# Loading the first fifteen pieces of two edge tables at stated counts of landed scatter groups

## The chip, the cores and the metric

The kernel runs on one core of a Trainium2 chip. The metric is the device time of one execution, in microseconds (us). The kernel before takes 2910.95 us, the median of 3 runs (2910.61 to 2911.79).

## The reference

Four stages stand one behind the other, each with a residual and a layer norm ahead of it: a graph network of three layers (SAGE with batch norm), an attention over learned slices, a hypergraph convolution, and a mixture of eight experts. The graph has 3125 nodes of 256 features and 53125 directed edges, sorted by target node. The change lies in the first graph layer, layer 0:

```python
for Wl, bl, Wr, g, b in params:
    agg = segment_sum(h[src], dst, N)
    deg = segment_sum(ones, dst, N)
    out = (agg / max(deg, 1)) @ Wl + bl + h @ Wr
    h = relu(batch_norm(out, g, b))
```

## The kernel before, in words

**Sums as products.** A neighbour sum h[src] by dst is a product of the features with a table of edge counts: 3200 x 3200 entries in fp16, source nodes by target nodes. The targets are split into five blocks of 640 (`NB` = 5, `BC` = 640), and a block of the table into five pieces (q = 0 to 4), each with the counts of 640 sources, 800 KB. The index n = 5b + q numbers the pieces through the blocks.

**Making the table.** There are two tables in DRAM, `at_counts` (even) and `odd_counts` (odd), so that two groups of scatters can be under way. VectorE works out, for groups of 512 edges, an address and a count for each (line 1147), and POOL writes them with DMAs that add one count per partition: four scatters of 128 make a group (`add_group`, line 602), even groups go to the even table, odd ones to the odd. There are 104 groups, 52 for each table. Ahead of a group of a table POOL waits until the table's previous group has landed (`pool.wait_ge(added, g // 2 * GROUP)`; `GROUP` = 64 is what one landed group adds to the semaphore `even_added` or `odd_added`). Since the edges are sorted by target, a block of the table is complete once a certain number of groups has landed.

**Using it.** SP's queue loads the pieces. `released(k, b)` reads the number of groups that block b needs, worked out from the edges by the kernel, and waits for it, once per table and block. Then for each piece `load_even(n)` fetches the even table's into `ring` (one of five slots; `chunk_used[q]` says that the slot is free, `sum_out` that what stood there was stored), and `load_odd(n)` the odd table's into one of two slots in `xrows` (`tables_summed` says that the slot is free). VectorE adds the two (`sum_tables`, line 1254), ACT's queue stores the sum back to the even table for the later layers (line 786), and TensorE multiplies (`aggregate`: degrees at line 1951, features at 1959). After a block's five pieces VectorE divides by the degrees (`aggregated`, lines 1213 to 1229), TensorE applies the weights (`mean_products`, line 1977) and VectorE adds and collects statistics (lines 1236, 1203).

**Order.** SP's queue loads nothing before all 104 groups have been worked out (`sp.wait_ge(idx_ready, NG)`), since `ring` holds the keys until then. All queues run in written order. VectorE's is: the five sums of block 0; then, for each block b, the sums n = 5(b+1) and 5(b+1)+1 of the next block, the division for block b, the sum of q = 2, the first of four additions, the sum of q = 3, the other three additions and the statistics, the sum of q = 4. TensorE enters block b+1 when the four additions of block b are done. The last block is loaded and used in three parts, each with its own release (targets 2560 to 2879, 2880 to 2996, and the rest; lines 1261 to 1301 on VectorE, 2013 to 2041 on TensorE). Layer 1 begins when the last part has gone through the batch norm.

Of the kernel before, what the change touches and what calls it, by code (L numbers as in the profile page):

```python
# [12 lines left out]
NB = T // BT  # L13
# [21 lines left out]
CHECKS = 3  # L35
EARLY = 4
GROUP = GQ * 16
AROW = T * BC
SPREAD = 64
ZW = 2000  # L40
AHEAD = BT + 3
ASIZE = NB * P * AROW
EPS = 1e-5
# [61 lines left out]
def build(nc, x, src, dst, w, out):  # L105
    ctx = ExitStack()
    with ctx:
# [65 lines left out]
        tfeat = tarena[:, 0:4 * T * P].rearrange("p (f n) -> p f n", f=4)  # L173
        zeros16 = tarena[:, :].bitcast(fp16)[:, 0:AROW]
        deginv = late[:, :]
# [142 lines left out]
        compared, idx_ready, even_added, odd_added, tables_summed = map(sem, ("compared", "idx_ready", "even_groups_added", "odd_groups_added", "tables_summed"))  # L318
# [117 lines left out]
        def _(sp):  # L436
# [22 lines left out]
            def released(k, b):  # L459
                landed = sp.value_load(release[:, k, b:b + 1], min_val=GROUP, max_val=NG * GROUP)  # L460
                sp.nop(nofuse=True)
                sp.wait_ge((even_added, odd_added)[k], landed)
                sp.nop(nofuse=True)

            def load_even(n):
                b, q = n // NB, n % NB
                sp.wait_ge(chunk_used[q], b + 1)
                if n >= NB:
                    sp.wait_ge(sum_out[(n - NB) % 2], 16 * ((n - NB) // 2 + 1))
                sp.dma_start(chunk_flat[q], at[:, b, q * BT * BC:(q + 1) * BT * BC]).then_inc(chunk_in[q], 16)  # L470

            def load_odd(n):
                b, q = n // NB, n % NB
                if n >= 2:
                    sp.wait_ge(tables_summed, n - 1)
                sp.dma_start(odd_chunk[n % 2], odd[:, b, q * BT * BC:(q + 1) * BT * BC]).then_inc(odd_in[n % 2], 16)

            for b in range(NB - 1):
                released(0, b)
                released(1, b)  # L480
                for q in range(NB):
                    load_even(b * NB + q)
                    load_odd(b * NB + q)
# [80 lines left out]
        def _(pool):  # L564
# [31 lines left out]
            def add_group(g, table, added):  # L596

                pool.wait_ge(idx_ready, g + 1)
                if g >= 2:
                    pool.wait_ge(added, g // 2 * GROUP)  # L600
                for c in range(g * GQ, (g + 1) * GQ):
# [92 lines left out]
        def _(act):  # L694
# [11 lines left out]
            def clear(table, zeroed, b):  # L706
                act.dma_start(table[:, b, :].rearrange("p (k c) -> p k c", c=ZW), zeros16[:, 0:ZW].unsqueeze(1).to_broadcast([P, AROW // ZW, ZW])).then_inc(zeroed, 16)

# [196 lines left out]
            def block_sqrt(b):  # L905
                wait(ln_var, 5 + NB + b)
                tiles = slice(b * BT, b * BT + BT)
                nc.scalar.activation(ln_s[:, tiles], ln_r[:, tiles], ACT.Sqrt).then_inc(ln_std, 1)

            _, c_tps, c_tcp, c_xps, c_high, _ = conv  # L910

            def conv_copy(t, i, k):
# [84 lines left out]
        def _(dve):  # L997
# [9 lines left out]
            def step(ins):  # L1007

                o.mark(ins)
                o.settle()  # L1010
# [9 lines left out]
            o.mark(V.tensor_reduce(row_block, eflt[:, 3, :], AX.X, ALU.max))  # L1020
            step(V.tensor_scalar(ekeyT, eflt[:, 0, :], float(AROW), None, ALU.mult))
            step(V.scalar_tensor_tensor(out=ekeyT, in0=eflt[:, 2, :], scalar=float(BC - P * AROW), in1=ekeyT, op0=ALU.mult, op1=ALU.add))
            step(V.scalar_tensor_tensor(out=ekeyT, in0=eflt[:, 3, :], scalar=float(P * AROW - BC), in1=ekeyT, op0=ALU.mult, op1=ALU.add))
            V.tensor_tensor(ekeyT, ekeyT, eflt[:, 1, :], ALU.add).then_inc(keys_dve, 1)
# [92 lines left out]
            def block_releases():  # L1117
# [19 lines left out]
                step(V.tensor_tensor(release[:, 0, :], groups, odd_groups, ALU.subtract))  # L1137
                V.tensor_scalar(release[:, 0:2, :], release[:, 0:2, :], GROUP, None, ALU.mult).then_inc(keys_dve, 1)
                dve.wait_ge(keys_dve, 5)
# [686 lines left out]
        def _(pe):  # L1826
# [62 lines left out]
            def enter_block(l, b, tile_rows, weights, last=HB):  # L1889

                rows, _, lo = ent[l][0:3]
                for h, tiles in ((0, (0, 1)), (1, (2, 3, 4))):
                    for i in tiles:
                        pe.wait_ge(lo, b * BT + (2 if i == 4 else 1))
                        for f in range(4):
                            if i == tiles[0]:
                                pe.wait_ge(rows, b * 8 + (4 * h + f + 1))
                            ins = tile_rows(i, f)
                        ins.then_inc(ent[l][3], 1)
                    half_products(l, b, h, weights, HB if h == 0 else last)  # L1900
# [305 lines left out]
            def turned(b, i, rows, tps, tcp, base=0):  # L2206
# [5 lines left out]
                ins.then_inc(tps, 1)  # L2212

            c_rows, c_tps, c_tcp, c_xps, _, c_low = conv

            def conv_turn(t, i, k):
# [192 lines left out]
```

## Time and profile before

| | us |
|---|---|
| median of 3 timed runs | 2910.95 |
| lowest, highest | 2910.61, 2911.79 |
| profiled execution, span from first to last instruction | 2916.6 |
| TensorE (PE) busy | 2404.2 |
| VectorE (DVE) busy | 1066.9 |
| POOL busy | 874.0 |
| ACT busy | 450.7 |

The profile is of one further execution, and nothing of it but its span is given as a time; it isn't one of the three that were timed. A busy time is the sum over an engine's instructions; waiting, and the issuing of DMAs by SP and ACT, aren't in it. POOL's scatters are counted as busy while POOL issues them; how long the data take to land is seen only by what waits for them. "Granted clock" is TensorE's clock as a share of 2.4 GHz. In a timeline, "idle before" in brackets is the time that the engine stood still ahead of an instruction, with what ended it; "issue" means that nothing the profile shows was waited for.

### The profile page before, as it was taken

The page shows a single profiled execution, that of the slowest core. Times are in us where ns is not written, and L with a number is a line of the kernel's source. Part 1 is how long each engine was busy: PE and PEld are TensorE (multiplying, and loading weights), DVE is VectorE, ACT ScalarE, POOL GpSimd, SP SyncE. Part 2 cuts the span into 40 slices and gives each one's busy share as a digit, 9 for nine tenths or more (in the row PEclk, how much of TensorE's full clock was granted, in tenths as well). Part 3 has the DMA queues.
Part 4 walks back from the last instruction along what each step waited for, and adds up shares of the span by engine and source line. Part 5 has one row for each costly group of instructions (what it writes and reads, how often), then busy time and mean ns, then how long its engine had stood idle before and what let it go on. Part 6 is the DMA issues. An engine that isn't in the chain of part 4 may idle for free.

```text
span 2916.6 us, 40191 instructions
## 1 busy us (share of the span) xinstructions
PE 2404.2 (82%) x14486; PEld 1802.4 (62%) x14486; DVE 1066.9 (37%) x2860; ACT 450.7 (15%) x1226; POOL 874.0 (30%) x627
## 2 busy tenths in 40 slices
PE   5285555842859999999997888999999994999997
PEld 2151113531547776677774457888888884888886
DVE  7688885502321011112115745112210577111111
ACT  0030000000015000004104822000110002222221
POOL 6888887787830000000002310000000000233332
PEclk6595556975979999999998979999999997999999
DMA  9922226925460999960243000444344434577666
GB/s 339 298 1 0 0 1 201 294 12 169 67 188 0 227 275 246 194 200 0 75 157 113 1 1 1 137 145 136 124 136 149 153 119 139 168 206 213 208 190 175
DMA packets 297786, 397.77 MB, mean 136 GB/s; under 512 B 177974, under 2 KB 241229, under 8 KB 297611
## 3 DMA queue, kind: packets, MB, share of 16 engines
q1 hardware_dynamic: 115530, 268.24, 28.7%
q10 hardware_dynamic: 109760, 108.20, 13.5%
q0 software_dynamic: 72400, 20.04, 8.2%
q8 instruction: 61, 1.00, 0.1%
q14 instruction: 35, 0.28, 0.0%
HBM read 279.30 MB, written 99.82 MB: 130 GB/s over the span
## 4 chain that ended last, share of the span: by engine, by line
PE 61%; POOL 14%; DVE 8%; DMA 7%; issue 6%; ACT 2%; ACTq 1%; DVEq 1%; POOLq 0%; SPq 0%
PE ps L1959 13%; PE ps L2270 8%; PE ps L2271 8%; POOL odd_counts L602 7%; PE ps L2364 7%; PE ps L2355 7%; POOL at_counts L602 7%; PE ps L1886 4%; DMA odd_counts<-tarena 3%; PE ps L1977 3%; DVE late L1147 2%; DMA odd_counts<-harena 2%; PE ps L2090 2%; PE ps L2203 2%; PE ps L2226 2%
## 5 line engine op out<-in xcount | busy, mean ns | idle before, releaser
L2270 PE MATMUL ps<-harena,ring 128*128 128x257 f16 (+1 forms) x2500 | 551.5, 272 | 8.7 <-DVE harena L1553 3.8
L2271 PE MATMUL ps<-harena,ring 128*128 128x256 f16 x2500 | 551.3, 271 | 0.0
L1959 PE MATMUL ps<-ring,harena 128*128 128x320 f16 x3800 | 514.8, 298 | 5.8 <-DMA ring<-at_counts 4.3
L1959 PEld LDWEIGHTS ps<-ring,harena 128*128 128x128 f16 x3800 | 372.6, 98 | 144.6 <-DMA ring<-at_counts 5.0
L602 POOL DMA_INDIRECT at_counts<-harena x208 | 330.6, 1589 | 85.8 <-issue 78.4
L602 POOL DMA_INDIRECT odd_counts<-harena x208 | 328.9, 1581 | 78.9 <-issue 60.1
L1147 DVE SCALAR_TENSOR_TENSOR late<-ps,ring 128x512 f16<-128x512 f32 x416 | 287.3, 746 | 21.8 <-PE ps L1848 10.7
L1848 PE MATMUL ps<-harena,ident 104*128 104x512 f32 x208 | 186.5, 1014 | 116.2 <-DVE late L1147 115.2
L2270 PEld LDWEIGHTS ps<-harena,ring 128*128 128x128 f16 x2500 | 243.2, 97 | 44.8 <-DVE harena L1591 5.9
L2271 PEld LDWEIGHTS ps<-harena,ring 128*128 128x128 f16 x2500 | 241.8, 97 | 31.1
L1977 PE MATMUL ps<-feat,wl 128*128 128x320 f32 x448 | 127.4, 446 | 111.0 <-DVE feat L1229 109.9
L661 POOL IOTA harena<- 1x32 int32 x1 | 0.2, 164 | 727.1 <-DVE xrows L1665 727.1
L2364 PE MATMUL ps<-ring,harena 128*128 128x256 f32 x896 | 201.7, 382 | 9.7 <-ACT harena L989 6.2
L2355 PE MATMUL ps<-harena,ring 128*128 128x256 f32 (+1 forms) x1024 | 201.6, 355 | 1.2 <-DVE harena L1799 1.2
L1848 PEld LDWEIGHTS ps<-harena,ident 104*128 104x128 f32 x208 | 50.3, 286 | 246.1 <-DVE late L1147 230.7
L2364 PEld LDWEIGHTS ps<-ring,harena 128*128 128x128 f32 x896 | 167.6, 190 | 38.5 <-issue 17.0
L2355 PEld LDWEIGHTS ps<-harena,ring 128*128 128x128 f32 x1024 | 177.1, 192 | 22.3 <-issue 1.6
L1977 PEld LDWEIGHTS ps<-feat,wl 128*128 128x128 f32 x448 | 87.0, 196 | 149.7 <-issue 111.7
L636 POOL DMA_DIRECT2D wl<-L_ffn_W_out x1 | 0.7, 714 | 594.0 <-DVE feat L1229 594.0
L684 POOL DMA_INDIRECT x_sum<-harena x56 | 88.8, 1586 | 267.2 <-DVE harena L1809 230.1
L732 ACT ACTIVATE bn_k<-bn_k 128x4 f32<-128x4 f32 (+1 forms) x3 | 0.6, 205 | 1058.2 <-DVE bn_k L1349 1058.2
L989 ACT ACTIVATE harena<-ps,harena 128x256 f32<-128x256 f32 (+1 forms) x256 | 114.6, 448 | 310.8 <-PE ps L2355 304.8
(398 smaller groups left out, 2538.6 us busy)
## 6 DMA issues: line engine op xcount, KB each, us to landing
ring<-at_counts SPq DMA_DIRECT2D x145, 800.0 KB
ring<-L_ffn_W SPq DMA_DIRECT2D x64, 1024.0 KB, 5.1
ring<-ad_counts SPq DMA_DIRECT2D x50, 800.0 KB
at_counts<-tarena ACTq DMA_DIRECT2D x5, 4000.0 KB, 22.5
odd_counts<-tarena ACTq DMA_DIRECT2D x5, 4000.0 KB
at_counts<-ring ACTq DMA_DIRECT2D x25, 800.0 KB
ad_counts<-xrows ACTq DMA_DIRECT2D x25, 800.0 KB, 6.1
xrows<-odd_counts SPq DMA_DIRECT2D x20, 800.0 KB
```

What stands on the lines that cost most here:

```text
L602: nc.gpsimd.indirect_dma_start(out=table, out_offset=bass.IndirectOffsetOnAxis(ap=eidx[:, c:c + 1], axis=0), in_=evalue[:, c:c + 1], in_of ...
L684: nc.gpsimd.indirect_dma_start(out=x_sum, out_offset=bass.IndirectOffsetOnAxis(ap=to_row[:, j:j + 1], axis=0), in_=yrow[c % 2][:, i, :], i ...
L989: nc.scalar.activation(hT[s][:, k, 0:n], ps[:, k % 4, 0:n], ACT.Gelu, bias=evc[s][:, k:k + 1]).then_inc(e_gelu, 1)
L1147: ins = V.scalar_tensor_tensor(out=ejunk[q], in0=ps[:, LOOK + s, :], scalar=ekey[:, bass.ds(g + q, 1)], in1=eweight[:, GE - P - q * P:2 * ...
L1848: M(ps[:, LOOK + g % LOOK, :], ident[0:ER, g:g + 1].to_broadcast([ER, P]), ekeyT, start=True, stop=True).then_inc(keys_spread, 1)
L1886: ins = M(ps[:, 4 + n % 4, 0:c], weights[:, d, fo * P:(fo + 1) * P], feat[:, d, h * HB:h * HB + c], start=(d == 0), stop=(d == 3))
L1959: ins = M(ps[:, 2 * f + h, 0:c], part[:, t, (2 * k + f) * P:(2 * k + f + 1) * P], chunk[q][:, s, h * HB:h * HB + c], start=(t == 0 and par ...
L1977: ins = M(ps[:, k + h, 0:HB], wl2[:, d, fo * P:(fo + 1) * P], feat[:, d, h * HB:(h + 1) * HB], start=(d == 0), stop=(d == nfi - 1))
L2270: M(ps[:, i, 0:wide], lhs, hh[:, t, 0:wide], start=(t == 0), stop=False)
L2271: ins = M(ps[:, i, 0:F], lhs, hl[:, t, :], start=False, stop=(t == T - 1))
L2355: ins = M(ps[:, k % 4, 0:n * P], w1e[s][:, d, k * P:(k + 1) * P], xeT[s][:, d, 0:n * P], start=(d == 0), stop=(d == 1))
L2364: ins = M(ps[:, 4 + s, i * F:(i + 1) * F], hT[s][:, k, i * P:(i + 1) * P], w2e[s][:, k, :], start=(k == 0), stop=(k == EK - 1))
```

## The change

Each of the fifteen pieces of blocks 0 to 2 gets a wait of its own, for the even table ahead of `load_even(n)` and for the odd one ahead of `load_odd(n)`: 31 + 7n // 10 groups of that table must have landed. The waits of `released` stay. No instruction is added, taken away or moved on any engine; the pieces of blocks 3 and 4 are loaded as before.

```diff
 GROUP = GQ * 16
+PACE_FROM = 31
...
+            def pace(added, n):
+
+                if n < 3 * NB:
+                    sp.wait_ge(added, GROUP * (PACE_FROM + 7 * n // 10))
+
             def load_even(n):
                 b, q = n // NB, n % NB
+                pace(even_added, n)
                 sp.wait_ge(chunk_used[q], b + 1)
...
             def load_odd(n):
                 b, q = n // NB, n % NB
+                pace(odd_added, n)
                 if n >= 2:
                     sp.wait_ge(tables_summed, n - 1)
```

## Rows read from the trace of the kernel before

**Rows 1.** The page: the span, and the chain that ended last, by engine.
```profile
span 2916.6 us, 40191 instructions
...
PE 61%; POOL 14%; DVE 8%; DMA 7%; issue 6%; ACT 2%; ACTq 1%; DVEq 1%; POOLq 0%; SPq 0%
```

**Rows 2.** Busy time by stretch: engines, TensorE clock, DMA share, GB/s.
```profile
473.00:536.00 63.00, 47.09 (x286) 32.54 (x286) 28.36 (x25) 0.00 (x0) 40.87 (x24) 0.86 1.04 377
536.00:586.00 50.00, 47.39 (x316) 33.56 (x315) 24.53 (x25) 0.00 (x0) 41.91 (x24) 1.00 0.85 253
473.00:586.00 113.00, 94.48 (x600) 66.10 (x600) 52.88 (x49) 0.00 (x0) 82.78 (x48) 0.92 0.96 322
586.00:697.00 111.00, 29.39 (x217) 20.94 (x214) 0.00 (x0) 0.00 (x0) 92.97 (x60) 0.65 0.27 19
```

**Rows 3.** POOL timeline: start us, us, engine, line, operation, tiles [idle before, releaser].
```profile
472.99 1.56 POOL L602 DMA_INDIRECT at_counts<-harena  x1 [0.31 <-issue]
...
478.57 2.94 POOL L602 DMA_INDIRECT at_counts<-harena  x1 [0.30 <-issue]
...
505.48 1.55 POOL L602 DMA_INDIRECT odd_counts<-harena  x1 [7.26 <-DMA odd_counts<-harena]
...
574.54 3.19 POOL L602 DMA_INDIRECT at_counts<-harena  x1 [0.30 <-issue]
...
586.06 1.55 POOL L602 DMA_INDIRECT at_counts<-harena  x1 [0.30 <-issue]
...
697.52 1.55 POOL L602 DMA_INDIRECT odd_counts<-harena  x1 [0.30 <-issue]
...
717.82 1.55 POOL L602 DMA_INDIRECT odd_counts<-harena  x1 [4.19 <-DMA odd_counts<-harena]
...
829.54 1.55 POOL L602 DMA_INDIRECT odd_counts<-harena  x1 [0.30 <-issue]
```

**Rows 4.** POOL, 473 to 586 us, by table; then its waits, 536 to 590.
```profile
L602 POOL DMA_INDIRECT at_counts<-harena x24 | 41.8, 1743 | 11.4 <-issue 6.7 <-DMA at_counts<-harena 4.7
L602 POOL DMA_INDIRECT odd_counts<-harena x24 | 41.0, 1707 | 18.8 <-DMA odd_counts<-harena 12.4 <-issue 6.1 <-DMA at_counts<-harena 0.3
...
POOL odd_counts L602 <- DMA odd_counts<-harena: 1.0, 1, 1.0
```

**Rows 5.** VectorE timeline: sums of an even and an odd piece.
```profile
478.26 1.82 DVE L1254 TENSOR_TENSOR ring<-ring,xrows 128x3200 f16<-128x3200 f16 x1 [4.79 <-DMA xrows<-odd_counts]
...
574.49 1.81 DVE L1254 TENSOR_TENSOR ring<-ring,xrows 128x3200 f16<-128x3200 f16 x1
...
697.85 1.83 DVE L1254 TENSOR_TENSOR ring<-ring,xrows 128x3200 f16<-128x3200 f16 x1 [113.52 <-DMA xrows<-odd_counts]
```

**Rows 6.** SP timeline: first and last load of blocks 0 to 2, then block 3.
```profile
471.85 0.36 SPq L470 DMA_DIRECT2D ring<-at_counts  x1
...
572.83 0.33 SPq L476 DMA_DIRECT2D xrows<-odd_counts  x1
691.49 0.33 SPq L470 DMA_DIRECT2D ring<-at_counts  x1
```

**Rows 7.** TensorE timeline of layer 0.
```profile
488.62 1.52 PE L1951 MATMUL ps<-ring,ones 128*128 128x320 f16 x10
...
495.41 1.52 PE L1951 MATMUL ps<-ring,ones 128*128 128x320 f16 x10
...
710.71 11.28 PE L1977 MATMUL ps<-feat,wl 128*128 128x320 f32 x32 [95.32 <-DVE feat L1229]
...
778.09 1.49 PE L2013 MATMUL ps<-ring,ones 128*128 128x320 f16 x5 [10.52 <-DVE ring L1261]
779.38 5.09 PE L2022 MATMUL ps<-ring,harena 128*128 128x320 f16 x20
...
784.99 2.88 PE L2022 MATMUL ps<-ring,harena 128*128 128x320 f16 x20
...
839.38 0.69 PE L2013 MATMUL ps<-ring,ones 128*128 128x128 f16 x5 [23.14 <-DVE ring L1261]
```


## The prediction

> **What bounds the kernel now.** I read the profile in this order: the page's chain of waits, then the busy table by stretch, then the timelines of POOL, VectorE, SP and TensorE around the change. The profiled execution spans 2916.6 us; the median of the timed runs is 2910.95 us, 5.65 us less, and I take every difference over from the one to the other. TensorE has 61% of the chain that ended last and POOL 14% [rows 1]; POOL's work is the scatters of line 602. The change lies in the POOL part: until the last scatter has been issued at 829.54 us [rows 3] the chain follows POOL, and layer 0 can't end before the last group has landed.
>
> A scatter is a DMA of 128 elements that POOL issues in 1.55 us with 0.30 us between. From 586.06 to 697.52 us POOL issues 60 without a disturbance [rows 3], so one takes 111.46 / 60 = 1.858 us and a group of four 7.43 us. In that stretch the DMA engines are 27% busy, on average 19 GB/s [rows 2]. Group 60 (counted from 0, the 31st of the even table) begins at 472.99 us and group 72 at 586.06 us [rows 3]: 12 groups in 113.07 us where 12 x 7.43 = 89.16 us would do. **23.9 us are lost**, just while the pieces of blocks 0 to 2 are loaded, from 471.85 to 572.83 us [rows 6], at 322 GB/s [rows 2]. Two things cause it:
>
> - Some of the 48 issues last longer than the 1.55 us. They take 41.8 + 41.0 = 82.8 us [rows 4]; 48 x 1.553 us would be 74.5, so 8.3 us are too many. In the timeline ten issues are stretched. The worst two are 2.94 us at 478.57 and 3.19 us at 574.54 [rows 3]. VectorE's sum of two pieces (line 1254, both inputs in SBUF, 1.82 us) ran from 478.26 and from 574.49 us [rows 5]. An issue that begins inside a sum is stretched by what is left of the sum, less about 0.12 us: 480.08 - 478.57 - 0.12 = 1.39, and 2.94 - 1.55 = 1.39. The other nine fit as well; one issue that began 0.02 us after a sum wasn't stretched.
> - POOL waits for an earlier group of the same table to land. 23.9 - 8.3 leaves 15.6 us for it; the idle time says the same, 11.4 + 18.8 = 30.2 us, of which 48 gaps of 0.30 are 14.4 and most of the rest stands beside the landings [rows 4]. All but 0.7 us comes before 536 us, at 377 GB/s; after that, at 253 GB/s [rows 2], a single wait remains, of 1.0 us against the usual gap of 0.30 [rows 4].
>
> **The change.** It adds waits on SP's queue and nothing else: no instruction, byte or sum more or less. Even piece n waits for 31 + 7n//10 even groups, odd piece n for as many odd ones: 31, 31, 32, 33, 33, 34, 35, 35, 36, 37, 38, 38, 39, 40, 40. Behind a waiting piece SP holds the later pieces, and for them wait VectorE's sums, TensorE's products and ACT's stores; POOL waits for none of these, only for its own landings. At 471.85 us POOL is in group 59, so 30 even groups have been issued: every threshold still lies ahead, and the change does bind. The first piece moves little: even group 31 lands about 482 us and odd group 31 about 489 us (issue end plus some 1.6 us, as where the loads of block 3 go at 691.49 us [rows 6] after the issue of their last group, which ends at 689.8 us). The first sum goes from 478.26 to about 494 us. The last piece of block 2 needs the 40th odd group, group 79: 472.99 + 20 x 7.43 = 621.6 us plus what POOL has lost by then, some 10 us, so about 633 us instead of 572.83. The same 36 MB then move in some 150 us instead of 113, near 240 GB/s.
>
> Term 1, the **waits for landings**. They need a long burst: the first loads go at 471.85 us and the long wait ends at 505.48; in block 3 the loads go at 691.49 and the wait ends at 717.82 [rows 3, 6]. Both come over 20 us after saturation began, since a group may take nearly 7.4 us to land before its table's next group is due. With the thresholds there is never more than three loads and two stores together (two pieces share a threshold at n = 0, 3, 6, 10 and 13), 4 MB, or 10 to 12 us. So I let the 15.6 us go. Put back: at 253 GB/s 0.7 us came in 6.3 groups, so in 20 groups between 0 and 2.3 us; I take 1.2.
>
> Term 2, the **sums**. All fifteen stay, and now each meets a POOL that is issuing. Before, four or five fell wholly or partly into POOL's waits. An issue begins every 1.858 us, a sum lasts 1.82, so nearly always one issue begins inside it and loses, with even phases and 1.82 - 0.12 = 1.70 us at stake, 1.70 x 1.70 / (2 x 1.858) = 0.78 us on average. Fifteen cost 11.7 us. The phases aren't independent, for the pieces are released by POOL's own landings: the bounds are 15 x 0 and 15 x 1.7 = 25.5 us, and 0.4 to 1.2 us each (6 to 18 us) is what I allow.
>
> The Trainium skill (SBUF — State Buffer, "Who interferes with whom") says that a VectorE instruction with two SBUF inputs contends with a GpSimd instruction that reads SBUF, but that a tensor_tensor wasn't seen to stall the writing of DMA descriptors. The trace bears out the first half and not the second: ten stretched issues, each begun inside a sum. By the second half term 2 would be nothing, which is the first rival.
>
> Term 3, **everything behind**. Block 3 is released by even and odd group 43, and the parts of block 4 by later ones, none of them paced. Their burst at 697 us, sums and waits included, is taken over unchanged, only earlier. With a gain G, layer 0's last release, and the rest of the program, come G earlier if TensorE isn't late. **Is it?** A piece costs it 6.79 us at full clock (488.62 to 495.41 [rows 7]); the pieces arrive every 0.7 x 14.9 = 10.4 us, 52 us a block, against 34 us of sums and some 12 us of weight products. But VectorE takes pieces n = 8 and n = 13 in the middle of its work on the block before, so TensorE enters block 1 about 575 us and block 2 about 643 us. It ends block 2 near 678 us; the first sum of block 3 (697.85 us before [rows 5]) falls near 686. VectorE turns to block 2's sums only after the second sum of block 3, near 693 us, so TensorE has 15 us in hand there, and its idle time before block 2's weight products, 95.3 us, shrinks to about 20. Behind it stand another 10.5 us before part 0 of block 4 and 23.1 us before part 2 [rows 7]. It costs nothing; the cover is 15 + 10.5 + 23.1, some 49 us.
>
> The sum: 23.9 - 11.7 - 1.2 = **11.0 us** less. 2910.95 - 11.0 = **2900.0 us**.
>
> **The rivals.**
> First, sums don't hurt POOL, and the stretched issues come from the loads as well. Then all 23.9 us go: 2887 us. Against it: in ten of ten cases the stretch fits the end of a sum to 0.02 us or so. For it: only the rule above. Chance 0.05.
>
> Second, the waits follow from the volume and not from its density: thirty loads and fifteen stores cost POOL the same wherever they lie, and fewer sums hide in waits. 15.6 us of waits come back: 23.9 - 11.7 - 15.6 is -3.4, a time between 2908 and 2914 us. For it: block 3's five pairs made a wait too. Against it: 536 to 586 us, 253 GB/s and one short wait. Chance 0.12.
>
> Third, slower: TensorE becomes late. Its place is blocks 2 and 3 of layer 0 and the first part of block 4. The gaps between paced pieces let its granted clock fall; it is 0.65 on average from 586 to 697 us, with 95 us of idleness [rows 2, 7]. Twenty products took 5.09 us after a 10.5 us pause and then 2.88 us [rows 7], which is the lower and the higher of the two levels, 1.2 and 2.4 GHz. If blocks 2 and 3 ran wholly at the lower one, 2 x 34 us more would be due, and 5 x 2.2 = 11 us in part 0: 79 us, 30 more than the cover of 49, less the gain of 11: 2930 us. It decides from 49 us of lateness on. Against it: those rows show the clock back within one piece, and a late TensorE has no gaps. Chance 0.03.
>
> Fourth, the phases are bad: each sum comes just before an issue, as at 574.49 us. 15 x 1.64 = 24.6 us, no gain, 2911 us. Chance 0.04. That leaves 0.76 for the forecast.
>
> **How the numbers follow.** The forecast's own range is 23.9 - 18 - 2.3 = 3.6 to 23.9 - 6 - 0 = 17.9 us of gain: 2893 to 2907. I widen it by 1 us on both sides for block 3's wait, which may fall otherwise: 2892 to 2908. The rivals at 2887 and 2930 and most of the second lie outside, together under 0.2. What a measurement of this kernel can tell from no change is 0.2%, 5.8 us. A gain above it: nine tenths of the forecast and all of the first rival, with a bit of the second, 0.77. Within it: 0.17. Slower by more, the third rival and a tail of the second: 0.06.
>
> **What would show it.** Right: the first load goes at 482 us and the first odd one near 489 instead of 471.85; POOL's waits for landings between 473 and 640 us total under 3 us over the normal gaps; about fifteen issues longer than 1.55 us, each begun inside a sum, together 8 to 15 us; the last scatter begins about 818.5 us instead of 829.54; TensorE's idle time before block 2's weight products falls to some 20 us and all later stages keep their lengths. Wrong: waits of 4 us or more in the paced stretch (second rival), no stretched issues (first), issues stretched by 1.4 us and more each (fourth), or TensorE working up to a part's release in block 4 so that VectorE waits for products there and not for a DMA (third).

## The result, and the profile after

The changed kernel takes 2896.28 us (median of 6 runs, 2894.0 to 2899.16), the kernel before 2911.37 us (median of 6 runs, 2909.23 to 2924.12; three of them are those given above). The ratio is 0.9948, 95% interval [0.9934, 0.9961]: 15.1 us or 0.5% faster. The ratios leave out one execution in a slower state of the chip (2958.05 us, with the wide thresholds; without it their median of 2913.44 us would be 2913.07). Two further sets of runs of the changed kernel, below, gave 0.9935 and 0.9952.

The page after the change answers to [rows 1]:

```profile
span 2894.1 us, 40209 instructions
...
PE 61%; POOL 19%; issue 7%; DVE 6%; DMA 3%; ACT 2%; ACTq 1%; DVEq 0%; POOLq 0%; SPq 0%
```

TensorE's share of the chain is unchanged, POOL's has grown from 14% to 19%, and DMA's has fallen from 7% to 3%. Only a small part of that comes from the change. Between 472 and 587 us landings of scatters had 37% of the chain before, 42 us or 1.5% of the span, and have nothing of it now: there the chain runs along POOL's own issues. The larger part lies between 88 and 257 us, which the change doesn't touch: the chain ran there along DMAs and VectorE before, without POOL, and runs 74% along POOL now. Nor did it follow POOL all the way to the last scatter before the change, as the prediction says; that holds from 257 us on, and with the landings counted as POOL's. The page counts 18 instructions more, though none was to be added; on TensorE, VectorE, ACT and POOL the counts are the same, so the rest fits SP's new waits.

The two spans differ by 22.5 us, more than the medians. Some 4 us of that isn't the change's: on the page before, TensorE's products of line 1959 waited 4.3 us for loads into `ring`, in layer 1, which nothing in the change touches, and in the execution after they didn't. Layer 1 itself begins 15.6 us earlier. At 1328 us (before) the two executions are 23.0 us apart: the same products took 2.7 us more in all (514.8 against 512.1 us), besides the 4.3 us of waiting.

**The stretch in question** runs to 640 us instead of 586. Busy time by stretch, as in [rows 2] (TensorE products and weight loads, VectorE, ACT, POOL, then TensorE's granted clock, the DMA share, GB/s):

```profile
473.00:536.00 63.00, 32.41 (x215) 21.99 (x216) 9.20 (x5) 0.00 (x0) 53.25 (x33) 0.75 0.73 209
536.00:640.00 104.00, 61.09 (x348) 41.72 (x346) 39.09 (x36) 0.00 (x0) 87.85 (x54) 0.81 0.76 218
473.00:640.00 167.00, 93.51 (x560) 63.72 (x561) 48.29 (x41) 0.00 (x0) 141.10 (x86) 0.79 0.75 215
```

215 GB/s over 167 us stand against 322 over 113. POOL's line now, by table, to be read against [rows 4] (its line 602 has become 610):

```profile
L610 POOL DMA_INDIRECT at_counts<-harena x44 | 71.2, 1618 | 13.4 <-issue 13.4
L610 POOL DMA_INDIRECT odd_counts<-harena x42 | 70.7, 1683 | 12.8 <-issue 12.8
```

No landing ends any of the idle time: all of it is "issue", 0.30 us for each of 86 scatters. The issues themselves took 71.2 + 70.7 = 141.9 us where 86 x 1.553 would be 133.6.

Timelines of POOL, answering to [rows 3], and of VectorE, answering to [rows 5]:

```profile
524.10 3.00 POOL L610 DMA_INDIRECT at_counts<-harena  x1 [0.30 <-issue]
...
556.55 3.03 POOL L610 DMA_INDIRECT at_counts<-harena  x1 [0.30 <-issue]
...
568.19 1.55 POOL L610 DMA_INDIRECT at_counts<-harena  x1 [0.31 <-issue]
...
683.38 1.55 POOL L610 DMA_INDIRECT odd_counts<-harena  x1 [0.30 <-issue]
...
702.88 1.55 POOL L610 DMA_INDIRECT odd_counts<-harena  x1 [3.55 <-DMA odd_counts<-harena]
...
814.30 1.55 POOL L610 DMA_INDIRECT odd_counts<-harena  x1 [0.30 <-issue]
```

```profile
493.27 1.90 DVE L1262 TENSOR_TENSOR ring<-ring,xrows 128x3200 f16<-128x3200 f16 x1 [20.85 <-DMA xrows<-odd_counts]
...
523.84 1.82 DVE L1262 TENSOR_TENSOR ring<-ring,xrows 128x3200 f16<-128x3200 f16 x1 [12.61 <-DMA xrows<-odd_counts]
...
556.33 1.82 DVE L1262 TENSOR_TENSOR ring<-ring,xrows 128x3200 f16<-128x3200 f16 x1 [12.65 <-DMA xrows<-odd_counts]
...
683.59 1.82 DVE L1262 TENSOR_TENSOR ring<-ring,xrows 128x3200 f16<-128x3200 f16 x1 [37.21 <-DMA xrows<-odd_counts]
```

Group 72 begins at 568.19 us instead of 586.06, group 87 at 683.38 instead of 697.52, and the last scatter goes at 814.30 us, 15.24 us earlier. Two of the longest issues, 3.00 us at 524.10 and 3.03 at 556.55, begin 0.26 and 0.22 us into a sum. The prediction's rule, that an issue is stretched by what is left of the sum less 0.12 us, gives 2.99 and 3.03; it fits all eleven stretched issues up to group 86 to 0.01 us. The wait in block 3's burst is still there: 3.55 us at 702.88, 4.19 before.

SP's loads (first even, first odd, last odd of block 2, first of block 3), answering to [rows 6], and TensorE, answering to [rows 7]:

```profile
481.39 0.36 SPq L477 DMA_DIRECT2D ring<-at_counts  x1
488.77 0.36 SPq L484 DMA_DIRECT2D xrows<-odd_counts  x1
...
631.82 0.38 SPq L484 DMA_DIRECT2D xrows<-odd_counts  x1
677.10 0.33 SPq L477 DMA_DIRECT2D ring<-at_counts  x1
```

```profile
582.16 1.53 PE L1959 MATMUL ps<-ring,ones 128*128 128x320 f16 x10 [1.09 <-DVE tarena L1244]
...
643.30 1.53 PE L1959 MATMUL ps<-ring,ones 128*128 128x320 f16 x10 [1.09 <-DVE tarena L1244]
...
696.44 10.42 PE L1985 MATMUL ps<-feat,wl 128*128 128x320 f32 x32 [19.01 <-DVE feat L1237]
...
763.05 1.49 PE L2021 MATMUL ps<-ring,ones 128*128 128x320 f16 x5 [10.60 <-DVE ring L1269]
...
824.04 0.69 PE L2021 MATMUL ps<-ring,ones 128*128 128x128 f16 x5 [21.87 <-DVE ring L1269]
```

TensorE enters block 1 at 582.16 and block 2 at 643.30 us, stands 19.01 us before block 2's weight products instead of 95.32, and 10.6 and 21.9 us before parts 0 and 2 of block 4 (10.5 and 23.1 before).

For the experiments I split POOL's losses by the timeline: a **stretch** is what an issue takes beyond 1.553 us, a **wait** what a gap has beyond 0.30 us. Sums in us, for groups 59 to 86 (loads of blocks 0 to 2, and the clean part behind them) and 87 to 103. Of each wait in the first column some 0.7 us is nothing but the third decimal of 112 gaps; after the change no single gap there is over 0.35 us:

| | stretch, wait, groups 59 to 86 | stretch, wait, 87 to 103 | last scatter at |
|---|---|---|---|
| before | 8.29, 16.44 | 3.70, 4.35 | 829.54 |
| after | 10.01, 0.68 | 3.26, 3.68 | 814.30 |

### The profile page after: what moved, and what is told of

Same layout as the page of the kernel before. It is cut to its first block, busy times and chain, and to the rows that moved or that the text cites. A ratio compares the mean times of both kernels' runs of the same rounds, so it can differ in the third digit from the quotient of the medians.

```text
span 2894.1 us, 40209 instructions
## 1 busy us (share of the span) xinstructions
PE 2405.5 (83%) x14486; PEld 1803.6 (62%) x14486; DVE 1066.9 (37%) x2860; ACT 450.2 (16%) x1226; POOL 874.8 (30%) x627
## 4 chain that ended last, share of the span: by engine, by line
PE 61%; POOL 19%; issue 7%; DVE 6%; DMA 3%; ACT 2%; ACTq 1%; DVEq 0%; POOLq 0%; SPq 0%
PE ps L1967 14%; POOL odd_counts L610 9%; POOL at_counts L610 9%; PE ps L2278 8%; PE ps L2279 8%; PE ps L2372 7%; PE ps L2363 7%; PE ps L1894 4%; PE ps L1985 3%; DMA odd_counts<-tarena 2%; PE ps L2098 2%; PE ps L2211 2%; PE ps L2234 2%; PE ps L2144 1%; ACTq L723 1%
## 5 line engine op out<-in xcount | busy, mean ns | idle before, releaser
L1967 PE MATMUL ps<-ring,harena 128*128 128x320 f16 x3800 | 512.1, 297 | 1.4 <-ACT tarena L769 0.8
## 6 DMA issues: line engine op xcount, KB each, us to landing
at_counts<-tarena ACTq DMA_DIRECT2D x5, 4000.0 KB, 22.5
```

Source lines behind the costliest of these rows:

```text
L1967: ins = M(ps[:, 2 * f + h, 0:c], part[:, t, (2 * k + f) * P:(2 * k + f + 1) * P], chunk[q][:, s, h * HB:h * HB + c], start=(t == 0 and par ...
```

## The experiments

Eleven runs were made, in three sets; the kernel before took 2913.48, 2910.80 and 2911.26 us (medians) in them.

### Late, but still in one burst

```diff
-                    sp.wait_ge(added, GROUP * (PACE_FROM + 7 * n // 10))
+                    sp.wait_ge(added, GROUP * PACE_FROM)
```

> The changed kernel with every threshold of the fifteen pieces at 31 groups: the loads start as late as with the change, but then go in one burst as before. My theory (what counts is how densely the loads lie): POOL's waits for landings between the first load and the end of the burst come back, 10 to 17 us where the change has under 1, and the time is that of before, 2908 to 2913 us. Rival (it is the later start that helps, or fewer loads beside the other traffic): waits stay under 3 us and the time near 2896 us.

Measured: 2911.27 us, ratio 1.0004 [0.9966, 1.0042]. POOL's waits for landings, 473 to 640 us (total, times, longest):

```profile
POOL odd_counts L610 <- DMA odd_counts<-harena: 9.1, 2, 5.9
POOL at_counts L610 <- DMA at_counts<-harena: 5.8, 2, 4.0
```

Waits of groups 59 to 86 are 14.4 us and stretches 8.8, the last scatter goes at 827.12 us. With the later start alone it goes 2.4 us earlier than before, which the times don't show; the rest of the gain comes from the spreading. The waits come ahead of groups 64 to 67: 1.5, 3.0, 3.8 and 5.6 us. The first, short one ends at 504.29 us, 15 us after the burst proper begins (the first odd piece goes at 488.84), the second at 516.51, after 28 us.

### Sums of 64 columns

```diff
-V.tensor_tensor(chunk_flat[q], chunk_flat[q], odd_chunk[n % 2], ALU.add).then_inc(tables_summed, 1)
+V.tensor_tensor(chunk_flat[q][:, 0:64], chunk_flat[q][:, 0:64], odd_chunk[n % 2][:, 0:64], ALU.add).then_inc(tables_summed, 1)
```

> The changed kernel with VectorE's sums of whole pieces cut to the first 64 of 3200 columns; most counts of the odd table are left out. My theory (an issue of POOL that begins inside a sum is stretched to its end): the stretched issues of blocks 0 to 3, 12 us together with the change, fall to under 1.5 us, and the time to 2883 to 2888 us. Rival (the loads stretch the issues and the sums only happen to stand beside them): 8 to 12 us of stretching remain, time 2894 to 2898 us.

Measured: 2886.82 us, ratio 0.9904 [0.9878, 0.9931]. POOL by table, 473 to 640 us:

```profile
L610 POOL DMA_INDIRECT at_counts<-harena x47 | 72.9, 1552 | 14.3 <-issue 14.3
L610 POOL DMA_INDIRECT odd_counts<-harena x44 | 68.3, 1552 | 13.4 <-issue 13.4
```

The mean issue is 1552 ns for both tables: with the same loads and landings, nothing is stretched (0.03 us in groups 59 to 86). The sums make the stretches. Part of the gain is given back in block 3, whose burst now costs 7.4 us of waits instead of 3.7: with the sums short the pieces can follow each other faster, which would explain it. The run with 0.99 us instructions in place of the sums, below, has 6.6 us there, but no run shows the cause by itself.

### Sums in quarters

```diff
-V.tensor_tensor(chunk_flat[q], chunk_flat[q], odd_chunk[n % 2], ALU.add).then_inc(tables_summed, 1)
+for c in range(0, BT * BC, BT * BC // 4):
+    part = slice(c, c + BT * BC // 4)
+    ins = V.tensor_tensor(chunk_flat[q][:, part], chunk_flat[q][:, part], odd_chunk[n % 2][:, part], ALU.add)
+ins.then_inc(tables_summed, 1)
```

> The changed kernel with each sum of a whole piece done as four instructions of 800 columns, same result. If POOL gets its turn between two instructions of VectorE, a stretch lasts at most one quarter: about 0.04 us for each quarter on average, some 3 us in all for 20 sums instead of 12, and the time is 2886 to 2890 us. Rival (four instructions back to back hold POOL off like one): stretching stays at 10 to 13 us, time 2895 to 2898 us.

Measured: 2887.39 us (6 runs, 2886.07 to 2887.59), ratio 0.9905 [0.9884, 0.9927]. Two sums on VectorE, the issue of POOL that begins inside each, and POOL's lines:

```profile
497.91 2.03 DVE L1264 TENSOR_TENSOR ring<-ring,xrows 128x800 f16<-128x800 f16 x4 [2.04 <-DMA xrows<-odd_counts]
...
510.79 2.03 DVE L1264 TENSOR_TENSOR ring<-ring,xrows 128x800 f16<-128x800 f16 x4 [10.85 <-DMA xrows<-odd_counts]
```

```profile
499.46 1.91 POOL L610 DMA_INDIRECT odd_counts<-harena  x1 [0.30 <-issue]
...
510.95 1.84 POOL L610 DMA_INDIRECT odd_counts<-harena  x1 [0.30 <-issue]
```

```profile
L610 POOL DMA_INDIRECT odd_counts<-harena x44 | 71.0, 1615 | 13.4 <-issue 13.1 <-DMA at_counts<-harena 0.3
L610 POOL DMA_INDIRECT at_counts<-harena x45 | 70.0, 1554 | 13.7 <-issue 13.4 <-DMA odd_counts<-harena 0.3
```

The issue at 499.46 us begins in the last quarter, 1.55 us into the four, and is 0.36 us too long: 499.94 - 499.46 - 0.12, as a whole sum would have made it. The one at 510.95 us tells the two apart. It begins in the first quarter, 0.16 us into the four; held to the end at 512.82 us it would take 3.30 us, and it takes 1.84. Stretches in groups 59 to 86 fall to 3.40 us, from 10.01. Other phases don't explain that: if every issue that begins inside four quarters had been held to their end, this very run would have 11.1 us. POOL does get its turn between two instructions of VectorE; the rival, that four back to back hold it off like one, is out. The price is 0.21 us more of VectorE for a sum (2.03 against 1.82), where it has idle time.

### Thresholds further apart

```diff
-                    sp.wait_ge(added, GROUP * (PACE_FROM + 7 * n // 10))
+                    sp.wait_ge(added, GROUP * (PACE_FROM + 11 * n // 10))
```

> The changed kernel with thresholds 31 + 11n//10 (31 to 46 groups) instead of 31 + 7n//10, so that the last piece of block 2 is asked for some 90 us later. Theory: the loads stay harmless to POOL, but TensorE, which has about 19 + 10.6 + 21.9 = 51 us of idle time in hand behind block 2, becomes late: the idle times before block 2's weight products and before parts 0 of block 4 go to nearly 0, and the time is 2900 to 2912 us. Rival (there is more cover than that, or block 3's loads catch up): 2893 to 2898 us.

Measured: 2913.44 us, ratio 0.9993 [0.9962, 1.0024]. POOL by table, 473 to 720 us, and TensorE from its entry into block 2 on:

```profile
L610 POOL DMA_INDIRECT at_counts<-harena x68 | 105.6, 1552 | 20.7 <-issue 20.7
L610 POOL DMA_INDIRECT odd_counts<-harena x66 | 102.7, 1557 | 20.1 <-issue 20.1
```

```profile
709.44 1.53 PE L1959 MATMUL ps<-ring,ones 128*128 128x320 f16 x10 [1.09 <-DVE tarena L1244]
...
745.08 8.85 PE L1985 MATMUL ps<-feat,wl 128*128 128x320 f32 x32 [1.51 <-DVE feat L1237]
...
790.70 8.85 PE L1985 MATMUL ps<-feat,wl 128*128 128x320 f32 x32 [1.54 <-DVE feat L1237]
803.03 0.85 PE L2021 MATMUL ps<-ring,ones 128*128 128x320 f16 x5 [3.48 <-DVE ring L1269]
...
841.27 0.69 PE L2021 MATMUL ps<-ring,ones 128*128 128x128 f16 x5 [2.51 <-DVE ring L1269]
...
858.24 2.96 PE L2064 MATMUL ps<-ident,feat 128*128 128x128 f32 x8 [4.92 <-ACT feat L759]
```

Two things happen at once. POOL does better than ever: mean issues of 1552 and 1557 ns, the last scatter at 804.62 us, 9.7 us before the changed kernel's. But TensorE enters block 2 at 709.44 instead of 643.30 us, 66 us late, goes through blocks 2 and 3 with pauses of 1.5 us at most, has 3.5 and 2.5 us left where it stood 10.6 and 21.9, and enters layer 1 at 858.24 instead of 841.89 us. The cover is finite, as the third rival had it, and 66 us exceed it: 16.4 us of them arrive at the end of layer 0. The time is 17 us above the changed kernel's; I had put it at 4 to 16, so a little too low.

### Block 3 paced as well, sums in quarters

```diff
                 if n < 3 * NB:
                     sp.wait_ge(added, GROUP * (PACE_FROM + 7 * n // 10))
+                else:
+                    sp.wait_ge(added, GROUP * (43 + (n - 3 * NB) // 2))
```

> The changed kernel with the sums in quarters and with waits for the five pieces of block 3 as well: 43, 43, 44, 44 and 45 groups. Theory: the wait of some 3.3 to 3.9 us that the burst of block 3 causes goes, and TensorE's 10.6 us of idle time behind block 3 cover the later pieces; the time is 3 to 4 us under that with quarters alone, so 2882 to 2885 us. Rival (block 3 has no slack, TensorE's products come late and the gain is given back in block 4): 2887 us or more.

Measured: 2883.62 us (6 runs, 2882.36 to 2885.26), ratio 0.9893 [0.9851, 0.9935], the fastest version of all. Where block 3's burst had made POOL wait, and its last scatter:

```profile
700.34 1.63 POOL L612 DMA_INDIRECT at_counts<-harena  x1 [0.30 <-issue]
...
803.05 1.55 POOL L612 DMA_INDIRECT odd_counts<-harena  x1 [0.30 <-issue]
```

Waits from group 87 on are 0.43 us, all of it rounding, instead of 4.44 with quarters alone, and stretches 1.00 instead of 2.18. Against quarters alone that makes 3.8 us less, by the medians of two sets of runs.

### The kernel before, with sums in quarters

> The kernel before, no paced loads, with the sums in quarters. The stretched issues fall from 8.3 + 2.4 us to about 3 us. If both losses stand side by side, the time falls by 6 to 8 us against before, to 2903 to 2906 us. Rival (a faster POOL only runs into the next wait for a landing, since the burst bounds the groups): waits grow by what the stretches lose, and the gain is 0 to 3 us.

The edit is that of the quarters, made in the kernel before. Measured: 2903.00 us, ratio 0.9967 [0.9941, 0.9993], 7.8 us under the kernel before. Stretches fall to 2.51 and 2.45 us, waits are 17.48 and 4.11. The two losses stand nearly side by side; a faster POOL runs only 1 us further into the waits.

### One input instead of two

```diff
-V.tensor_tensor(chunk_flat[q], chunk_flat[q], odd_chunk[n % 2], ALU.add).then_inc(tables_summed, 1)
+V.tensor_scalar(chunk_flat[q], chunk_flat[q], 1.0, None, ALU.mult).then_inc(tables_summed, 1)
```

> The changed kernel with VectorE's sum replaced by a product with 1 of the even piece alone, one input in SBUF, in place; the odd table's counts are left out. If the second SBUF input makes the conflict, the stretches vanish and POOL's last scatter is issued near 804 us. Rival (any fast instruction of VectorE on fp16 between SBUF and SBUF holds POOL off): stretches remain, about as long as the instruction that makes them.

This kernel too leaves the odd table's counts out. One execution: 2894.26 us, the last scatter at 811.44 us (of which 2 us are a later first scatter, 26.29 us instead of 24.23). The theory that the second input alone does it fell:

```profile
495.38 0.99 DVE L1262 TENSOR_SCALAR ring<-ring 128x3200 f16<-128x3200 f16 x1 [22.64 <-DMA xrows<-odd_counts]
499.47 1.31 DVE L1262 TENSOR_SCALAR ring<-ring 128x3200 f16<-128x3200 f16 x1 [3.10 <-DMA xrows<-odd_counts]
```

```profile
498.93 1.94 POOL L610 DMA_INDIRECT odd_counts<-harena  x1 [0.30 <-issue]
```

The instruction takes 0.99 us instead of 1.82, and stretches still total 3.36 us in groups 59 to 86, most of them 0.39 us. In this pair both sides lose: the issue began at 498.93 us, ahead of VectorE's at 499.47, and took 1.94 us, while VectorE's took 1.31 instead of 0.99. So this one-input instruction on fp16 collides with POOL too, and in another way, since an issue that is already running is lengthened too (six of the seven, begun 0.54 to 0.97 us ahead of the instruction; the seventh, at 640.71 us, began inside it and fits the rule for sums). From this one run alone I can't say how the two divide the loss.

### A landing for each piece, one and a half groups apart

```diff
+            def last_group(n):
+                return 61 + 3 * n // 2
...
+                    groups = last_group(n) + 1
+                    sp.wait_ge(added, GROUP * ((groups + 1) // 2 if added is even_added else groups // 2))
...
+                    if n < 3 * NB and last_group(n) % 2 == 0:
+                        load_odd(n)
+                        load_even(n)
+                    else:
...
```

> The changed kernel, whole sums again, but piece n completed by the landing of group 61 + 3n//2 and of no other piece's: its last load starts at that landing alone. In the run with thresholds 31 + 11n//10, where each piece had a landing of its own, every sum of blocks 0 to 2 ended as POOL's next issue began, and 15 sums stretched the issues by 0.3 us together. If that phase is what counts, stretching of blocks 0 to 2 is 0.3 to 4 us (7.7 and 10.5 with the change), waits for landings under 2 us, and the time 6 to 10 us under the changed kernel's: 2885 to 2890 us. Rival (the phase is lost again through the stores and the two loads that go together, or mattered little): 7 to 12 us of stretching and 2893 to 2898 us.

Measured: 2896.40 us, ratio 0.9946 [0.9931, 0.9960]; stretches of groups 59 to 86 9.37 us. The expectation was missed, and its rival (7 to 12 us of stretching, 2893 to 2898 us) came true. In the run with wide thresholds a sum began 4.5 to 4.6 us after its odd piece had been asked for (607.37 to 611.95, 622.21 to 626.69, 651.97 to 656.55, 666.84 to 671.47 us), each time as the last part of POOL's group was passing. Here the time from the last request to the sum is 4.8, 5.7, 4.6, 5.8, 4.4 and 6.0 us for the first six pieces, in turn short and long. With a period of 1.86 us, one microsecond is the whole difference between missing POOL and hitting it. The phase counts, but it is lost when the pieces come closer. Why the time varies here no run shows; that more loads and stores run together than with wide thresholds may be the reason.

### Two pieces for each pair of groups, in short bursts

```diff
-                    sp.wait_ge(added, GROUP * (PACE_FROM + 7 * n // 10))
+                    sp.wait_ge(added, GROUP * (PACE_FROM + n // 2))
```

> The changed kernel with thresholds 31 + n//2 (31 to 38): two pieces for each pair of groups, 4.8 MB every 14.9 us, 322 GB/s on average, as in the kernel before. If POOL waits only after some 20 us of saturation on end, the waits before block 3 stay at 0 to 4 us. Rival (the mean density decides): 8 to 16 us of waits, as before. TensorE isn't nearer to being late in either, so the time is that of the changed kernel plus the waits: 2895 to 2900 us, or 2904 to 2911 us.

Measured: 2900.21 us, ratio 0.9961 [0.9946, 0.9976]. POOL by table, 473 to 640 us:

```profile
L610 POOL DMA_INDIRECT at_counts<-harena x44 | 72.7, 1653 | 13.6 <-issue 13.3 <-DMA odd_counts<-harena 0.3
L610 POOL DMA_INDIRECT odd_counts<-harena x41 | 70.6, 1722 | 12.5 <-issue 12.2 <-DMA at_counts<-harena 0.3
```

Waits are 0.89 us, next to nothing beyond the rounding. By stretch, as in [rows 2]: this kernel over 113 us and in one burst, then the kernel before in and around block 3's burst, then the late burst:

```profile
489.00:602.00 113.00, 82.12 (x527) 56.67 (x528) 38.87 (x30) 0.00 (x0) 95.74 (x57) 0.85 0.92 283
492.00:504.00 12.00, 7.69 (x47) 5.16 (x48) 3.65 (x2) 0.00 (x0) 9.87 (x8) 0.70 1.08 365
```

```profile
605.00:718.00 113.00, 17.68 (x95) 12.16 (x94) 14.46 (x10) 0.00 (x0) 91.45 (x59) 0.58 0.42 88
692.00:718.00 26.00, 7.29 (x18) 4.91 (x19) 14.46 (x10) 0.00 (x0) 18.77 (x12) 0.55 1.07 380
```

```profile
489.00:545.00 56.00, 41.85 (x266) 29.20 (x267) 22.78 (x14) 0.00 (x0) 35.55 (x23) 0.86 1.06 386
```

The loads paused from 559 to 576 us, and the mean over 113 us is 283 GB/s instead of the 322 of before ([rows 2]), so the density isn't quite that which cost 16.4 us. In this run bursts of 12 us at 365 GB/s, with slower stretches between (261 GB/s from 504 to 519 us), made POOL wait for nothing; 56 to 63 us at 377 to 386 cost 14 to 16 us. Block 3's burst in the kernel before says over what time to look: 26 us at 380 GB/s cost 3.9 us (the gap of 4.19 at 717.82 us, [rows 3]) although the mean over the 113 us up to it is only 88 GB/s, where 283 cost nothing here. So it isn't the mean of the stage that counts, but what happens within some 25 us: 26 us at 380 GB/s cost something, 12 us didn't, and neither did 30 us at 300 GB/s (579 to 609 us here, DMA share 0.98). No run has short bursts that aren't started by POOL's own landings, so what that timing adds isn't known. The time was expected at 2895 to 2900 us and lies 0.2 us above that. Against the changed kernel of the same set (2894.24 us) it is 6 us longer, though the two intervals overlap; stretches up to group 86 are 11.44 us instead of 7.0 there, all fifteen sums meeting an issue.

### The changed kernel again, twice

> The changed kernel again, on this chip and beside these, as the measure for them: 2894 to 2899 us, POOL's last scatter issued near 814 us, 10 to 12 us of stretched issues in blocks 0 to 3, under 1 us of waits for landings before block 3.

Measured: 2894.72 us, ratio 0.9935 [0.9913, 0.9958]; stretches 7.0 us up to group 86 and 6.4 behind, waits 0.72 before block 3, the last scatter at 815.29 us.

> The changed kernel again, beside these two: 2894 to 2899 us.

Measured: 2894.24 us, ratio 0.9952 [0.9933, 0.9970]; stretches 7.0 and 4.3 us, waits 0.71, the last scatter at 814.12 us.

## Why the prediction was right

2900.0 us were forecast and 2896.28 measured; 11.0 us of gain and 15.1. Sign and mechanism held, and both terms that it rests on were separated on the chip.

**Where the first loads and the last go.** 482, 489 and 633 us were given; 481.39, 488.77 and 631.82 us they are.

**Term 1, the waits.** I let 15.6 us go and put 1.2 back, net 14.4. They fell from 16.44 to 0.68 us, so 15.8, and what is left is rounding. The reason given was that a long wait needs some 20 us of saturation before it. One late burst brings 14 us of waits back (a first, short one after 15 us), and bursts of some 12 us bring none at 283 GB/s over 113 us, while block 3's 26 us at 380 bring 3.9 with a mean of 88. So the length of a stretch at the full rate of 365 to 380 GB/s is borne out, as lying between 12 and 26 us; 30 us at 300 GB/s still cost nothing. The 1.2 us put back was a term too many: no gap up to group 86 in the three executions of the changed kernel was over 0.35 us. The single wait between 536 and 586 us wasn't a rate that carries over; that it belonged to the tail of the burst is my reading.

**Term 2, the sums.** That they stretch POOL's issues is shown by the run that cuts them to 64 columns and by the one in quarters. The size was given as 11.7 us for fifteen sums (0.78 each). Stretches of groups 59 to 86 were 10.01, 7.00 and 7.01 us in three executions of the changed kernel, 0.47 to 0.67 us for a sum and 8.0 us on average: the term was 3.7 us too large. In the profiled execution itself, 4.2 us more were gained than forecast (15.24 against 11.0): 1.7 from this term (11.7 against 10.0), 1.4 from term 1 and 1.0 in block 3, whose losses I had taken over unchanged. Even phases was the assumption that failed. In the execution shown four of the fifteen sums cost nothing, because one issue began with them, or within 0.14 us, and the next at their end. Phases follow from POOL's own landings, as the text said without using it for the value: 15 sums cost 0.3 us with wide thresholds, and 11.4 with the denser ones. That the sum of the terms came out near the measured time is therefore in part luck: the same arithmetic would give these two kernels the same 11.7 us. The range of 0.4 to 1.2 us each holds the three executions, but not the wide thresholds.

**Term 3, everything behind.** The last scatter moved by 15.24 us: 14.0 of it before group 87 (lost time 23.9 before, 9.9 after), 1.0 in block 3's burst, the other 0.2 in small pieces. Layer 1 begins at 841.89 instead of 857.53 us. TensorE was expected in block 1 at 575 us (582.16), in block 2 at 643 (643.30), at its end near 678 (677.4), with 20 us left before the products (19.01).

**The rivals.** The first (sums do no harm) falls with the short and the quarter sums. The Trainium skill (SBUF — State Buffer, "Who interferes with whom") says of tensor_tensor that it takes only the read side of what the two engines share, and infers from this why it wasn't seen to stall a DMA; here a tensor_tensor with two SBUF inputs stretched the issue of an indirect DMA by up to 1.64 us, and the measurement decides. The second (waits follow the volume) falls with the late burst against the changed kernel: same volume, 14.4 against 0.7 us. The third (TensorE late) didn't happen with 7n//10 but does with 11n//10, where 66 us of lateness cost 16.4. By that the cover is 66 - 16 = 50 us or so, where the prediction had 49. The two are not made of the same parts: TensorE's waits before block 2's weight products and the three parts gave 45 us, and the rest came from products that ran faster after shorter pauses (block 2's weight products in 8.85 us instead of 10.42). The rival's other half, that the granted clock would stay at the lower level, had no part in it: the pieces ran at 6.8 us throughout. The fourth (bad phases) wasn't met in any run; the worst was 0.76 us a sum, with thresholds 31 + n//2.

## What to carry to other kernels

When an engine issues small transfers and waits for earlier ones to land, spread the bulk loads beside it, and look at the length of the stretches at the full rate rather than at the mean of the stage; then check how late the consumer may become, for what exceeds its idle time arrives at the end (16.4 of 66 us here). Where the timeline shows that an instruction of one engine holds off another engine's, and the loss is what remains of the one that is running, cut the long one into pieces, if its engine has time to spare. A gain worked out with even phases should keep a wide range where one engine's events set the other's.

## What the runs showed of the hardware that wasn't expected

Four VectorE instructions back to back cost POOL far less than one of the same length (3.4 against 7.0 to 10.0 us over fifteen sums). What an issue and a sum that begin almost together do to each other turns on some 0.05 us. In all runs with whole sums, an issue that began up to 0.04 us after the sum wasn't stretched, and the sum took up to 1.90 us instead of 1.82 (493.31 after 493.27 us in the changed kernel); one that began 0.05 us or more after it was held to the end, 1.64 us in the worst case (574.54 after 574.49 us in the kernel before). A one-input instruction on fp16 between SBUF and SBUF, 0.99 us long, was itself lengthened to 1.31 us by a running issue, which no two-input sum was by more than 0.08 us.
